# A transformer block on one core: every matmul of attention and its projections on half-precision pairs, scaled by factors found on the chip

## The reference

```
h = layernorm(x)
q, k, v = h @ Wq + bq, h @ Wk + bk, h @ Wv + bv        # each 1024 x 4096: 32 heads of 128
q, k = rms_norm(q) * gq, rms_norm(k) * gk              # over all 4096 values of a token
attn = softmax(q k^T / sqrt(128)) per batch and head   # 512 x 512
x = x + layernorm((attn @ v) @ Wo + bo)
h = layernorm(x)
ffn = h @ W_base^T + b_base + 2 * (gated low-rank experts: 8 experts of rank 16)
out = x + layernorm(ffn)
```

## Time and profile before

| what | us |
|---|---|
| median of 3 runs | 1155.52 (1154.96 to 1159.28) |
| the profiled execution | 1156.69 |
| its span, first to last instruction | 1154.9 |
| PE busy | 1116.7 |
| DVE busy | 803.0 |
| ACT busy | 675.2 |
| POOL busy | 575.5 |
| mean granted TensorE clock | 0.992 of full speed |

### The profile page before, as it was taken

The page is one execution under the profiler, slowest core; times in us unless marked ns, Lnnn a source line. Parts: engine busy times, 40 slices in busy tenths (PEclk is TensorE's granted clock), DMA queues, the critical chain, the costliest instruction groups (busy, mean ns, idle before and its releaser), DMA issues.

```text
span 1154.9 us, 17917 instructions
## 1 busy us (share of the span) xinstructions
PE 1116.7 (97%) x5704; PEld 881.6 (76%) x5704; DVE 803.0 (70%) x1336; ACT 675.2 (58%) x1331; POOL 575.5 (50%) x296
## 2 busy tenths in 40 slices
PE   6999999999999689999999999999999999999896
PEld 5888888888888567777777777777777777777575
DVE  6364554554554668778778787787777877877786
ACT  4343333333342766777777777777677677776532
POOL 2544444444457745555556555565565555554322
PEclk9999999999999899999999999999999999999999
DMA  5543433434435588798696776777878778887701
GB/s 187 200 161 131 163 138 134 163 132 141 163 127 183 103 172 169 173 173 165 166 182 153 177 170 156 184 163 154 175 173 164 165 173 171 162 155 127 195 1 73
DMA packets 307582, 179.62 MB, mean 156 GB/s; under 512 B 272096, under 2 KB 274272, under 8 KB 303328
## 3 DMA queue, kind: packets, MB, share of 16 engines
q1 hardware_dynamic: 307552, 179.25, 63.6%
HBM read 76.45 MB, written 35.66 MB: 97 GB/s over the span
## 4 chain that ended last, share of the span: by engine, by line
PE 90%; DVE 3%; DMA 2%; ACT 2%; SPq 1%; issue 1%; POOL 0%; DVEq 0%; ACTq 0%
PE ps L844 30%; PE ps L845 30%; PE ps L846 30%; ACT ps L687 1%; DMA wa_stage<-w_qk 1%; DMA pair_k<-pair_q 1%; ACT pair_q L696 0%; DVE pair_q L1314 0%; PE ps L854 0%; DVE stats L1124 0%; SPq L361 0%; DVE neg_max L1300 0%; DMA qk_in<-x 0%; DMA y<-x 0%; SPq L391 0%
## 5 line engine op out<-in xcount | busy, mean ns | idle before, releaser
L478 POOL TENSOR_TENSOR qk_lo<-qk_in,qk_hi 128x1024 fp32r<-128x1024 f32 x64 | 153.5, 2399 | 248.5 <-ACT qk_hi L655 248.5
L432 POOL TENSOR_TENSOR acc<-acc,squares 128x1024 f32<-128x1024 f32 x60 | 143.8, 2399 | 182.5 <-ACT squares L598 182.5
L1314 DVE SCALAR_TENSOR_TENSOR pair_q<-ps,row_inv,pair_q 128x512 f16<-128x512 f32 x256 | 174.5, 744 | 84.2 <-ACT pair_q L696 77.6
L687 ACT ACTIVATE ps<-ps,neg_max 128x512 f32<-128x512 f32 x256 | 168.6, 658 | 84.7 <-DVE neg_max L1300 84.7
L598 ACT ACTIVATE squares<-ps,q_k_bias 128x512 f32<-128x512 f32 x128 | 88.0, 690 | 212.8 <-PE ps L846 212.4
L1195 DVE TENSOR_SCALAR qk_out<-ps,tab 128x512 f32<-128x512 f32 x128 | 102.9, 807 | 150.3 <-ACT squares L598 150.3
L844 PE MATMUL ps<-xh,wa_hi 128*128 128x512 f32 x512 | 200.0, 391 | 1.5 <-DVE xl L1179 1.4
L846 PE MATMUL ps<-xh,wa_lo 128*128 128x512 f32 x512 | 199.2, 389 | 0.0
L845 PE MATMUL ps<-xl,wa_hi 128*128 128x512 f32 x512 | 199.2, 389 | 0.0
L1300 DVE TENSOR_REDUCE neg_max<-ps 128x1 f32<-128x512 f32 x256 | 167.0, 684 | 10.0 <-PE ps L846 8.2
L846 PE MATMUL ps<-wv_hi,xl 128*128 128x256 f32 (+1 forms) x544 | 158.3, 291 | 0.0
(11 more groups left out here) (127 smaller groups left out, 2124.4 us busy)
## 6 DMA issues: line engine op xcount, KB each, us to landing
q_k_scratch<-qk_out SPq DMA_DIRECT2D x32, 1024.0 KB, 4.7
qk_in<-q_k_scratch SPq DMA_DIRECT2D x64, 512.0 KB, 4.6
wa_stage<-w_qk SPq DMA_DIRECT2D x32, 512.0 KB, 5.5
wv_stage<-w_v SPq DMA_DIRECT2D x16, 512.0 KB, 5.0
wo_stage<-w_o SPq DMA_DIRECT2D x16, 512.0 KB, 5.2
y<-x SPq DMA_DIRECT2D x8, 256.0 KB, 5.4
y<-bo SPq DMA_DIRECT2D x8, 256.0 KB, 4.1
pair_k<-pair_q SPq DMA_TRANSPOSE x128, 4.7
```

What stands on the lines that cost most here:

```text
L432: pool.tensor_tensor(acc[:, w, :], acc[:, w, :], squares[:, par, w, :], ALU.add).then_inc(acc_ready, 1)
L478: pool.tensor_tensor(qk_lo[:, s % 2], qk_in[:, s], f32(qk_hi[:, s % 2]), ALU.subtract).then_inc(qk_lo_ready, 1)
L687: act.activation(ps[:, SCORE + i, :], ps[:, SCORE + i, :], ACT.Exp, bias=neg_max[:, sl, i:i + 1], accum_out=row_sum[:, sl, i:i + 1]).then_ ...
L1314: dve.scalar_tensor_tensor(out=pair_q[:, 1, i, :], in0=ps[:, SCORE + i, :], scalar=row_inv[:, sl, i:i + 1], in1=pair_q[:, 0, i, :], op0=AL ...
```

## The change

All operands of q, k, v, the scores and the output projection become `float16` pairs. So that they fit into its range, each gets a factor. Those of x and of the normed q and k are constants (`X_UP`, `QK_UP`); those of the weights are found on the chip from the largest absolute weight, now for Wq and Wk of every head, for Wv and for Wo of every pair; one for gq by gk of every head is found once. The softmax's exponential undoes the factor of q and k with its scale. The feed-forward part stays as it is, in tensors of its own (`zh`, `zl`).

The weights of q and k get four load slots. For head h+2 DVE takes the largest weights, SP stores 128 pairs of numbers to DRAM, waits for them, loads them back to all partitions, and DVE makes the factors in the next head:

```diff
-            def phase_a(i, by_batch=False, last=False):
-                for par in range(2):
-                    if not last:
-                        sp.wait_ge(wa_lo_ready, 2 * i + par + 1)
-                        load_wa(2 * i + 2 + par, par)
-                    sp.wait_ge(qk_out_ready, ...)
-                    sp.dma_start(q_k_scratch[...], qk_out[:, par])
+            def phase_a(i, o, by_batch=False, load=True, top=True):          # SP
+                h, par, pair = 4 * i + o, o % 2, 2 * i + o // 2
+                if load:
+                    if o or not by_batch:
+                        sp.wait_ge(wa_lo_ready, 2 * h)
+                    load_wa(h + 3, (o + 3) % 4)
+                if top:
+                    sp.wait_ge(qk_top_ready, h + 3)
+                    sp.dma_start(qk_top_scratch[bass.ds(h + 2, 1)]..., qk_top[:, par, :]).then_inc(qk_top_stored, 16)
+                    sp.wait_ge(qk_top_stored, 16 * (h + 1))
+                    sp.dma_start(qk_tops[:, :, :], qk_top_scratch[bass.ds(h + 2, 1)].broadcast_to(
+                        [P, P, 2])).then_inc(qk_tops_loaded, 16)
+                sp.wait_ge(qk_out_ready, ...)
+                sp.dma_start(q_k_scratch[...], qk_out[:, par]).then_inc(stored[par], 16)
...
+            for o in range(2):
+                phase_a(0, o, by_batch=True)
+            store_v_top(0)
+            load_v_tops(0)
+            store_o_top(0)
+            load_o_tops(0)
+            with sp.Fori(1, PAIRS // 2 - 1) as i:
+                for o in range(-2, 2):
+                    phase_a(i, o)
...
+            def next_factors(h, par):                                        # DVE
+                dve.wait_ge(qk_tops_loaded, 16 * (h - 1))
+                dve.tensor_reduce(qk_most[:, par, :], qk_tops[:, :, :]..., AX.X, ALU.max)
+                qk_factors(h, par)          # two small operations: down, then its reciprocal up
+                qk_columns(h, par)          # two more: the gain and the bias columns of the head
...
+            def phase_a(i, o, top=True):                                     # DVE
+                h, par = 4 * i + o, o % 2
+                next_factors(h + 1, 1 - par)
+                if top:
+                    largest_qk(h + 2, par, (o + 2) % 4, 16 * (i + (o + 2) // 4 + 1))
+                dve.wait_ge(stored[par], 16 * (2 * i + o // 2))
+                store_qk(par, 0, h, 4 * h + 1)
+                low_wa(h + 1, 1 - par, (o + 1) % 4)
+                dve.wait_ge(qk_cols_ready, 2 * h + 2)
+                for g in range(1, 4):
+                    store_qk(par, g, h, 4 * h + g + 1)
```

ACT's split of a head's weights goes from one pass over 1024 values to four over 512, each half first scaled in place:

```diff
+            def high_wa(h, par, slot):
+                act.wait_ge(qk_up_ready, h + 1)
+                for w in range(2):
+                    act.activation(wa_stage[:, slot, w], wa_stage[:, slot, w], ACT.Copy,
+                                   scale=qk_up[:, par, w:w + 1]).then_inc(wa_scaled, 1)
+                    act.wait_ge(wa_scaled, 2 * h + w + 1)
+                    act.activation(wa_hi[:, par, w], wa_stage[:, slot, w], ACT.Copy).then_inc(wa_hi_ready, 1)
```

In a step of attention the maxima are multiplied by the score's factor, two at a time, before the exponentials may use them; the split of an attention output moves from ACT and DVE to POOL; and a weight is scaled by POOL before its low part is taken:

```diff
+            def maxima(n, h, sl):                                            # DVE
+                for i in range(0, TB, 2):
+                    maximum(n, sl, i)
+                    maximum(n, sl, i + 1)
+                    scale_maxima(n, h, sl, i)     # 128x2, waits for both maxima
...
             def step(p, s, par, ...):                                        # DVE
-                for i in range(TB):
-                    maximum(n, sl, i)
-                    if i == 1 and output:
-                        evacuate_o((s - 2) % 4, n - 2)
+                maxima(n, 2 * p + sl, sl)
+                if factors:
+                    if s == (2 if first else 1):
+                        value_factors(p + 1, 1 - par)
+                    if s == 3:
+                        out_factors(p + 1, 1 - par)
                 inverses(n, sl)
...
+                if s == 3 and after:
+                    largest_value(p + 2)
+                if s == 1 and factors:
+                    largest_out(p + 1)
...
+            def split_o(s, n):                                               # POOL, first in its step
+                pool.wait_ge(o_t_ready, n + 1)
+                pool.tensor_copy(oth[:, sl, cols], o_t[:, sl, :]).then_inc(oth_ready, 1)
+                pool.wait_ge(oth_ready, n + 1)
+                pool.tensor_tensor(otl[:, sl, cols], o_t[:, sl, :], oth[:, sl, cols], ALU.subtract)
...
             def split_weights(hi_ready, lo_ready, count, lo, stage, hi, up, done):   # POOL
                 pool.wait_ge(hi_ready, count)
-                pool.tensor_tensor(lo, stage, f32(hi), ALU.subtract).then_inc(lo_ready, 1)
+                pool.tensor_scalar(stage, stage, up, None, ALU.mult).then_inc(w_scaled, 1)
+                pool.wait_ge(w_scaled, done)
+                pool.tensor_tensor(lo, stage, hi, ALU.subtract).then_inc(lo_ready, 1)
...
             def step(p, s, ...):                                             # SP
+                    if s == (1 if first else 0):
+                        store_v_top(p + 1)
+                    if s == 2:
+                        store_o_top(p + 1)
                 sp.wait_ge(high_ready, 4 * n + 4)
                 sp.dma_start_transpose(...high half...)
+                if more:
+                    if s == (1 if first else 0):
+                        load_v_tops(p + 1)        # waits for the store to have landed
+                    if s == 2:
+                        load_o_tops(p + 1)
                 sp.wait_ge(low_ready, 4 * n + 4)
                 sp.dma_start_transpose(...low half...)
```

More of the change, by code:

```diff
@@ L35, with build @@
 P = 128
-def build(nc, x, w_qk, w_v, w_o, tables, bo, w_base, w_in, b_t, b_base, b_thr, out):
+def build(nc, x, w_qk, w_v, w_o, tables, gains, bo, w_base, w_in, b_t, b_base, b_thr, out):
     NT = x.shape[0]
@@ L194, in build @@
         xl_ready = sem("xl_ready")
-        wa_loaded = [sem("wa_loaded0"), sem("wa_loaded1")]
+        wa_loaded = [sem(f"wa_loaded{slot}") for slot in range(4)]
         wa_hi_ready = sem("wa_hi_ready")
@@ L320, in load_qk @@
+            for o in range(-2, 1):
+                phase_a(PAIRS // 2 - 1, o)
+            phase_a(PAIRS // 2 - 1, 1, load=False)
             def load_qk(pair, s):
@@ L332, in _ @@
             sp.dma_start(wv_stage[:, :, :], w_v[1]).then_inc(wv_loaded, 16)
-            phase_a(PAIRS - 1, by_batch=True, last=True)
+            for o in range(2, 4):
+                phase_a(PAIRS // 2 - 1, o, by_batch=True, load=False, top=False)
             sp.wait_ge(stored[0], 16 * PAIRS)
@@ L531, in _ @@
             step(PAIRS - 1, 1, 1, weights=False)
+            step(PAIRS - 1, 2, 1, prepare=False, weights=False)
+            step(PAIRS - 1, 3, 1, prepare=False, weights=False)
             pool.wait_ge(ffn_hi_ready, 3)
@@ L1203, in _, with largest_value @@
                 if pos == 5:
[L1204 to L1207 removed]
+                    next_factors(2, 0)
+                    low_wa(2, 0, 2)
+                    largest_qk(3, 1, 3, 16)
+            def largest_value(pair):
                 dve.wait_ge(wv_loaded, 16 * pair + 16)
[L1210 to L1211 removed]
@@ L1241, in _ @@
+            with dve.Fori(1, PAIRS // 2) as i:
+                for o in range(-2, 2):
+                    phase_a(i, o)
             value_factors(0, 0)
+            out_factors(0, 0)
             def mean_squares(b, bank):
@@ L1355, in _ @@
             for s in range(4):
-                step(PAIRS - 2, s, 0)
+                step(PAIRS - 2, s, 0, after=False)
             step(PAIRS - 1, 0, 1, factors=False)
-            step(PAIRS - 1, 1, 1)
+            step(PAIRS - 1, 1, 1, factors=False)
             def add_x(t):
@@ L1445, in _ @@
             step(PAIRS - 1, 2, 1, rows=False, factors=False)
-            for i in range(TB):
-                maximum(N + 1, 1, i)
-                if i == 1:
-                    evacuate_o(1, N - 1)
+            maxima(N + 1, HEADS - 1, 1)
             inverses(N + 1, 1)
@@ L1556 @@
                            axis=1),
+        "gains": np.stack([np.asarray(v).reshape(heads, P) for v in (L0_attn_gq, L0_attn_gk)], axis=1),
         "bo": on_all(L0_attn_bo),
```

562 lines of the change are left out of this document (363 added, 199 removed).

## The result

The changed kernel takes 1358.6 us (median of four, 1356.9 to 1361.04) against 1155.24 (1153.16 to 1159.28) before: 1.1757 times, 95% interval 1.1719 to 1.1795. The prediction said 1388, with 1275 to 1480. The time lies in the range. The parts of the sum do not lie where I had put them, and that is what the experiments are about.

What follows compares the result with a forecast made beforehand. PE bounded the kernel, with DVE within half a microsecond a step in attention. From 1156.7 us, start and projection +176.5, attention +55 and the end +1 gave 1389, or 1388 as median, 20% slower; 80% range 1275 to 1480.

Steps and rivals of the forecast that it cites:

- Part 1: Matmuls everywhere: on float16, 512 columns fall from 0.227 to 0.2156 us and 256 columns from 0.120 to 0.108.
- Part 2: Projection loop: finding Wq and Wk factors through a store and load back takes 15.7 us a head, against 10.9 before.
- third rival: Projection loop: the store of 8-byte pieces is acknowledged quicker, 12.5 us a head, 1296 us in all; chance 10%.
- signs of being wrong: Stated refutations: heads 10.4 us apart, a small store landing in under 4 us, or no PE idle in attention.
- Part 3: Start: first products and factors come later, head 4's factors near 98 us; start and projection together cost 176.5 us more.
- Part 4: Attention: a step takes 11.9 us against about 11.0, +55 us over some 61 steps, bounds 0 and +100.
- a small scaling that waits for both: Attention step on DVE: scaling after the first two maxima, counted as finished 1.5 us after the first maximum starts.
- POOL's loop of 11.5 us: Attention step: the loop through ACT and POOL, 4.5 and 6.9 us, takes 11.5 us a step (10.7 to 12.3).
- Part 5: The end: the last two outputs each get one more ACT pass of 0.7 us, +1 us in all.
- The first: Rival: the round trip hides and PE is the limit, with store and load under 8.05 us; 1114 us, chance 4%.
- the second: Rival: the round trip decides in projection, but attention gets PE's gain; 1296 us, chance 12%.
- The fourth: Rival: PE's clock held at half by idling makes a projection head 20.7 us, +135, 1523 us; chance 5%.

Runs made afterwards that it cites:

- experiment 3: Changed kernel with the scratch for each head's largest Wq and Wk weights stored in 256 pieces of 4 bytes instead of 128 of 8: 1490.36 us.
- experiment 1: Changed kernel with DVE's two scalings of the softmax maxima per step, each on 128x2, made into four on 128x1: 1270.22 us.
- experiments 7: On top of 6, maxima over Wv and Wo moved into DVE's wait for the exponentials, their factors behind the row inverses, loads back behind the low transpose: 1248.72 us.
- 9: On top of experiment 1, a constant in place of the head's per-partition factor in the exponential: 1264.18 us.
- 10: On top of experiment 1, POOL's scaling of the staged Wv and Wo weights left out: 1259.97 us.
- 11: Changed kernel with the edits of experiment 1, experiment 4, 6, 7, 9 and 10, plus a constant bound replacing the Wq and Wk round trip: 1203.95 us.
- 12: On top of 11, the factors of Wv and Wo taken behind DVE's rows instead of ahead of its low halves: 1238.35 us.
- experiment 8: Kernel before the change, with only x, Wq, Wk, Wv and two feed-forward weights as float16 pairs and no factors: 1129.01 us, ratio 0.9761.
- 6: Changed kernel with the edits of experiment 1 and experiment 4, and v_top and y_down as one-input operations: 1268.01 us.
- experiment 4: Changed kernel with the first loads back of Wv's and Wo's largest weights moved behind the head loop, their stores issued without waits: 1348.09 us.

## Why the prediction was right, and where it was not

**Part 1** held: 0.216 and 0.109 for 0.2156 and 0.108.

**Part 2** failed in one term. The loop and its members were right, as experiment 3 shows. But I took the store's landing from the row with 4-byte pieces (8.4) and stretched the bounds only to 8.3, though I had named 2.1 as a far bound. The store has 8-byte pieces and lands in 3.8, and in 2.9 with nothing beside it. My third rival said this, at 10%, with 3.2 us less a head; it was 4.6 less, and 0.8 less for the load, which lets PE's time and the loop meet at 10.3. Heads 10.6 apart for 15.7, some 28 times, is the -140. Of the prediction's own signs of being wrong, a small store in under 4 us came, and heads 10.4 apart nearly (10.6).

**Part 3** held to some 7 us: PE's first product at 20 (21.8 measured), the second batch at 38 (39.4), the factors of heads 2, 3 and 4 at 52, 71 and 98 (51.3, 63.6 and 90.9), head 2 at 57 (54.9). The two 4-byte stores ahead of head 4 took 11.3 and 7.9 where I had 8.4 each; the 8-byte ones were quicker.

**Part 4** failed in the other direction: 162 us and not 55. The step it fails at is "a small scaling that waits for both", counted as an ordinary small operation. It waits for POOL and takes 1.08 us in the mean instead of 0.2, and ahead of the exponentials it lies on the path: 89 of the 162 us (first to last reciprocal, 856.0 to 767.3 in experiment 1). The evidence stood in the kernel before: its low part of Wq and Wk, two inputs from SBUF, took 2384 ns in the mean, but 1224 to 1227 in the four cases in which it began with POOL idle; the reduction over as many values took 1209. It mostly began 0.9 us into an addition of POOL's and ended 1.1 us behind the end of that:

```profile
71.56 2.40 POOL L432 TENSOR_TENSOR acc<-acc,squares 128x1024 f32<-128x1024 f32 x1 [0.33 <-ACT squares L598]
72.46 2.58 DVE L1163 TENSOR_TENSOR wa_lo<-wa_stage,wa_hi 128x1024 fp32r<-128x1024 f32 x1
```

I hadn't asked why. Of the rest, the edits of experiments 7, 9 and 10 with those of 11 took 36 us, and 37 are left in the two steps of a pair in which the factors of Wv and Wo are made. Experiments 11 and 12 show two sides of it: with the factors early, DVE waits for the loads back; with them late, PE waits for the output. Whether an earlier load or another order on ACT and POOL would free it was not tried. POOL's loop of 11.5 us, which I took as the floor, was none: taking 1.57 us out of it gave 0.13 a step. And the limit that attention started from was PE alone (400.0 of 400 us busy, experiment 8), not PE and DVE within half a microsecond as the prediction had it.

**Part 5** said +1; 2.4 was measured.

**The rivals.** The first, PE the limit in the projection part, came true for the loop: store and load took 3.8 + 4.2 = 8.0 us, just under the 8.05 that it asks for. It did not for the start, and it had attention faster as well. That is also what the second had, and attention took 162 us longer. By the Trainium skill's "DMA: Bandwidth & Descriptors", section "Anatomy of one DMA", the prediction had 4.3 us for the round trip, about half of what the trace shows; that section is on DMAs that GpSimd issues, and SP issues these. The fourth, the clock: before head 4 PE had nothing for 16.6 us. Some 2 us into that the granted clock fell to 0.50, which is 1.2 GHz, and it stayed there for 20.5 us, until PE had worked for 5.9. The stretch with no work, and the stretch at half clock (length, busy us by engine, clock, DMA share, GB/s):

```profile
80.20:96.80 16.60, 0.00 (x0) 0.00 (x0) 4.15 (x10) 5.48 (x9) 0.61 (x1) 0.56 0.50 139
82.29:102.77 20.48, 5.89 (x14) 2.10 (x15) 9.61 (x18) 6.63 (x11) 5.14 (x2) 0.50 0.54 166
```

It didn't decide; the mean clock over the span was 0.978. In experiment 3, where PE does idle in every head, it was 0.941, and the heads came 15.05 apart, not the 20.7 of a clock held at half.

So the time was right by luck, through two misses of opposite sign, and the projection part and attention each lay outside the bounds that I had given them.

## What to carry to other kernels

A faster matmul type pays where PE alone is the limit and its operands need nothing new: 2.4% came from the types of the projections' operands alone (experiment 8); the changed kernel lost such a gain and 17.6% more by what its factors put on the other engines and on the round trips through memory. All types changed without the factors was not run. Before a small DVE operation goes onto the path beside a busy POOL, look at its form: one value with one input, or an operand in PSUM, costs 0.2 us; two values, or two inputs from SBUF, cost up to the whole of POOL's operation, and the profile books it as busy. Price a scattered store by how close its pieces lie, and price an edit by the path it lies on: five of my twelve expectations (6, 7, 9, 10, 12) took a duration or a wait for a gain.

## What the hardware showed that I had not expected

- A store of 128 pieces of 4 bytes lands in 7.3 us side by side and in 1.4 at 64 bytes apart; 8 bytes in 2.9 and 1.4. A store of 8-byte pieces behind two of 4-byte ones landed in 12.1 (experiment 4).
- DVE's multiplication by a factor for each partition, on two, three or four values, waits for POOL's running operation; on one value it doesn't (862 to 1477 ns against 214), and a copy of two values took 1821.
- The exponential takes 747 ns with a factor for each partition, 658 without (the row below against L687 in the kernel before).
- POOL's one-input scaling of 512 values by a factor for each partition takes 1565 ns, its two-input subtraction to float16 1159 (rows from 600 to 1100 us).

```profile
L823 ACT ACTIVATE ps<-ps,neg_max,exp_scale 128x512 f32<-128x512 f32 x256 | 191.1, 747 | 315.4 <-DVE neg_max L1565 315.4
```

```profile
L539 POOL TENSOR_SCALAR wv_stage<-wv_stage,v_up 128x512 f32<-128x512 f32 x19 | 29.7, 1565 | 26.8 <-ACT wv_hi L752 26.8
...
L541 POOL TENSOR_TENSOR wo_lo<-wo_stage,wo_hi 128x512 f16<-128x512 f32 x18 | 20.9, 1159 | 1.5
```
